# Gathering new and old cache rows in the other order, with filler rows in place of skipped ones

## The reference, cut to what matters

```
k = rope(rms(x @ Wk)), v = x @ Wv                     # 64 new rows for each sequence
k_blocks[block_of(pos), :, pos % 16] = k              # written into the paged cache
v_blocks[block_of(pos), :, pos % 16] = v
k_all, v_all = k_blocks[block_tables], v_blocks[block_tables]
scores = q . k_all / 16, allowed where pos - 256 < kpos <= pos
x = x + softmax(scores) @ v_all @ Wo
```

## Time and profile before

| | us |
|---|---|
| median of 3 runs | 442.44 |
| lowest and highest run | 441.16, 442.81 |
| span of the profiled execution | 494.4 |
| PE busy in it | 444.6 (90%) |
| DVE, POOL, ACT busy in it | 311.1, 268.9, 230.2 |
| DMA rate, mean over the span | 140 GB/s |
| q0, the queue of POOL's gathers | 22.08 MB, 16.5% of 16 engines |

### The profile page before, as it was taken

One profiled execution on the slowest core, in us unless ns is written; L12 is line 12 of the kernel. 1 busy time (PEld: TensorE's weight loads), 2 busy tenths in 40 slices (PEclk: granted clock), 3 DMA queues, 4 the chain that ended last, 5 costly groups with the idle time before them and its releaser, 6 DMA issues.

```text
span 494.4 us, 9866 instructions
## 1 busy us (share of the span) xinstructions
PE 444.6 (90%) x2890; PEld 320.9 (65%) x2890; DVE 311.1 (63%) x901; ACT 230.2 (47%) x590; POOL 268.9 (54%) x241
## 2 busy tenths in 40 slices
PE   5999999996898999989799989897979898989997
PEld 2434468453666777767577767685858675767776
DVE  4988885682646666747465757565647565666543
ACT  1322113653445555646355646554445554555541
POOL 2598157487364756555546556556555556554000
PEclk9999999999799999999989999999999999999999
DMA  6396859755346544453434445353534453434111
GB/s 199 109 302 197 296 170 288 271 144 167 85 110 179 141 115 143 115 147 99 136 100 142 113 143 129 111 147 106 149 88 122 123 141 82 123 104 109 47 54 44
DMA packets 76266, 69.08 MB, mean 140 GB/s; under 512 B 50516, under 2 KB 52692, under 8 KB 76214
## 3 DMA queue, kind: packets, MB, share of 16 engines
q1 hardware_dynamic: 57248, 42.03, 28.7%
q0 software_dynamic: 15456, 22.08, 16.5%
q10 hardware_dynamic: 3510, 4.35, 2.4%
HBM read 78.39 MB, written 11.93 MB: 183 GB/s over the span
## 4 chain that ended last, share of the span: by engine, by line
PE 71%; DVE 11%; issue 9%; ACT 4%; another core or an unknown queue 3%; DMA 2%; ACTq 0%; DVEq 0%; SPq 0%
PE banks L1112 27%; PE banks L1244 8%; PE banks L1125 7%; PE banks L1279 7%; PE banks L1252 5%; PE banks L1106 5%; PE banks L1264 5%; DVE prob L974 3%; DVE x L887 2%; PE banks L1226 2%; ACT x L662 2%; PE banks L1292 2%; DMA kvb<-kvl_dram 1%; PE banks L1378 1%
## 5 line engine op out<-in xcount | busy, mean ns | idle before, releaser
L514 POOL DMA_INDIRECT windows<-kvrows_dram,idx_all x78 | 82.6, 1059 | 63.7 <-PE banks L1264 29.0
L634 ACT ACTIVATE pt_s<-banks 112x384 f32<-112x384 f32 x128 | 57.7, 498 | 96.5 <-PE banks L1252 70.9
L514 POOL DMA_INDIRECT windows<-newkv,idx_all x78 | 79.4, 1019 | 27.6 <-issue 22.4
L974 DVE CUSTOM_DVE_ANT_0 prob<-banks,mask 128x336 f32<-128x336 f32 x128 | 58.5, 505 | 52.1 <-issue 22.4
L628 ACT ACTIVATE prob<-prob,negmax 128x336 f32<-128x336 f32 x128 | 72.4, 567 | 32.3 <-DVE negmax L974 18.3
L484 POOL TENSOR_TENSOR rstd<-ms,half 128x8 f32<-128x8 f32 x24 | 45.9, 1913 | 66.4 <-DVE ms L907 46.2
L1125 PE MATMUL banks<-wkv_s,xt_s 128*128 128x512 f32 x128 | 58.7, 616 | 5.6 <-DMA xt_s<-xt_dram 5.6
L1252 PE MATMUL banks<-cst,prob 128*112 128x128 f32 x384 | 52.7, 273 | 0.2
L1264 PE MATMUL banks<-pt_s,windows 112*64 112x128 f32 x624 | 41.8, 281 | 10.6 <-ACT pt_s L634 8.7
L1112 PE MATMUL banks<-wf_hi,x 128*128 128x512 f32 x120 | 41.7, 408 | 10.5 <-DVE x L887 10.5
L1244 PE MATMUL banks<-kt_s,qt_s 64*128 64x336 f32 x256 | 47.5, 471 | 2.8 <-issue 2.8
(11 more groups left out here) (212 smaller groups left out, 825.0 us busy)
## 6 DMA issues: line engine op xcount, KB each, us to landing
usel<-utab SPq DMA_DIRECT2D x64, 128.0 KB
xt_s<-xt_dram SPq DMA_DIRECT2D x31, 256.0 KB
newkv<-kvo SPq DMA_DIRECT2D x16, 256.0 KB
stage<-xtok_dram SPq DMA_DIRECT2D x16, 256.0 KB
tsel<-ttab SPq DMA_DIRECT2D x64, 64.0 KB
out_dram<-xo ACTq DMA_DIRECT2D x15, 256.0 KB
windows<-kvrows_dram,idx_all POOLq DMA_INDIRECT x78
windows<-newkv,idx_all POOLq DMA_INDIRECT x78
```

What stands on the lines that cost most here:

```text
L514: P.indirect_dma_start(kv_s[i][:, c, :], None, newkv if new else kvrows, bass.IndirectOffsetOnAxis(ap=idx_all[:, new * CH + c, b:b + 1], a ...
L634: A.activation(pt_s[g][:], tb[g % 2][0:KP, 0:CH * 128].rearrange("p (c q) -> p c q", c=CH), ACT.Copy).then_inc(S["pt_ev"], 1)
L974: V.tensor_tensor_reduce(out=prob[b % 3][:, g, :], in0=sbk[g][:, 0:WK], in1=mask[b % 2][:], scale=-1.0 / 16, scalar=3.0e38, op0=ALU.add, o ...
```

## The change

`index_rows` gives every old window row of the sequences 2 to 31 a filler index into `newkv` (a row number spread over that table by the block number) in place of an index out of bounds. For the sequences 0 and 1 (`EARLY`) the skipped rows stay. The old indices are as before, so the old gathers still skip the rows that are new. Since a filler row must be overwritten by the old one, the new half is issued first and the old half after it has landed, except for sequences 0 and 1. In iteration k POOL now waits for `pv_mm` to reach k, then waits until the new half of k + 3 has landed, and then issues the old half of k + 3 and the new half of k + 4 by turns; `root_query` follows in even iterations.

```
-                for i in range(2):
-                    h = slice(HR * i, HR * i + HR)
-                    w = bank[6 + i][0:BLOCK, 0:HR]
-                    has = (qrot, qt_s[0])[i][0:BLOCK, 0:HR]
-                    V.tensor_scalar(none[:, h], w, 0.0, float(NONE), ALU.is_equal, ALU.mult)
-                    link(V.tensor_scalar(has, w, 0.0, float(NONE), ALU.is_gt, ALU.mult))
-                    V.tensor_tensor(rows[:, 1, h], w, none[:, h], ALU.add)
-                    link(V.scalar_tensor_tensor(has, blkrow[0:BLOCK, h], float(BLOCK), has, ALU.mult, ALU.add))
+                parts = [(slice(HR * i, HR * i + HR), bank[6 + i][0:BLOCK, 0:HR], (qrot, qt_s[0])[i][0:BLOCK, 0:HR]) for i in range(2)]
+                for h, w, has in parts:
+                    V.tensor_scalar(has, w, 0.0, float(NONE), ALU.is_gt, ALU.mult)
+                    last = V.tensor_scalar(other[:, h], blkrow[0:BLOCK, h], SPREAD, con("off1", BLOCK), ALU.mult, ALU.add)
+                link(last)
+                first = other.rearrange("p (s b) -> p s b", b=NB)[:, :, 0:EARLY]
+                link(V.tensor_scalar(first, first, float(NONE), None, ALU.add))
+                for h, w, has in parts:
+                    V.scalar_tensor_tensor(other[:, h], w, 0.0, other[:, h], ALU.is_equal, ALU.mult)
+                    last = V.scalar_tensor_tensor(has, blkrow[0:BLOCK, h], float(BLOCK), has, ALU.mult, ALU.add)
+                link(last)
+                for h, w, has in parts:
+                    V.tensor_tensor(rows[:, 1, h], w, other[:, h], ALU.add)
                     last = V.tensor_scalar(rows[:, 0, h], has, con("off", BLOCK), None, ALU.add)
...
+            def half_landed(b):
+
+                pool.wait_ge(kv_in[b % WINDOWS], 96 * (b // WINDOWS) + 48)
...
-            gather(0, 1)
-            gather(1, 1)
-            gather(2, 0)
-            gather(2, 1)
-            gather(3, 0)
+            for b in range(EARLY):
+                half_landed(b)
+                for c in range(CH):
+                    gather(b, 1, c)
+            for b in range(EARLY, 4):
+                for c in range(CH):
+                    gather(b, 1, c)
+            half_landed(2)
+            for c in range(CH):
+                gather(2, 0, c)
...
-                    gather(4, 0)
-                    continue
-                if k + 2 < NB:
-                    gather(k + 2, 1)
-                if k + 4 < NB:
+                if k and k + 4 < NB:
                     pool.wait_ge(S["pv_mm"], k)
-                    gather(k + 4, 0)
-                if k % 2 == 0 and k // 2 + 1 < TILES:
+                if k + 3 < NB:
+                    half_landed(k + 3)
+                    for c in range(CH):
+                        gather(k + 3, 0, c)
+                        if k + 4 < NB:
+                            gather(k + 4, 1, c)
+                if k and k % 2 == 0 and k // 2 + 1 < TILES:
                     root_query(k // 2 + 1)
```

More of the change, by code:

```diff
@@ L26 @@
 SHIFT = 271
+EARLY = 2
+SPREAD = (NB * NT - BLOCK - 1) / (NPOOL - 1)
 WIN_COLS = 32 * WS
@@ L31 @@
 _WIDTHS = [[("ident", 128), ("same_batch", 128), ("of3", NE3)],
-           [("order", NW * NW * NB), ("off", 1), ("toff", NW * BLOCK), ("code", 1), ("ones", NB)],
+           [("order", NW * NW * NB), ("off", 1), ("off1", 1), ("toff", NW * BLOCK), ("code", 1), ("ones", NB)],
            [("inv", 32), ("tpos", 1), ("win", 1)]]
@@ L60, in constants @@
     put("off", np.arange(BLOCK)[:, None])
+    put("off1", np.arange(1, BLOCK + 1)[:, None])
     put("win", (NSLOT * b)[:, None])
@@ L129, in build @@
         later = part(NB, NW * NW * NB // 2, f16).rearrange("p (j n) -> p j n", j=NW)
-        none = blkd[0:BLOCK, 0:WIN_COLS]
+        other = blkd[0:BLOCK, 0:WIN_COLS]
         assert at[0] <= 4 * CH * 512
@@ L507, in _, with gather @@
             root("k", 6, 0)
-            def gather(b, new):
+            def gather(b, new, c):
                 i = b % WINDOWS
[L511 to L518, removed]
+                P.indirect_dma_start(
+                    kv_s[i][:, c, :], None, newkv if new else kvrows,
+                    bass.IndirectOffsetOnAxis(ap=idx_all[:, new * CH + c, b:b + 1], axis=0),
+                    bounds_check=NB * NT if new else NPOOL * BLOCK - 1, oob_is_err=False,
+                ).then_inc(kv_in[i], 16)
+            def half_landed(b):
+                pool.wait_ge(kv_in[b % WINDOWS], 96 * (b // WINDOWS) + 48)
             root("k", 7, 0)
@@ L522, in _ @@
             root("q", 1, 1)
-            gather(0, 0)
+            for c in range(CH):
+                gather(0, 0, c)
             root("k", 8, 0)
-            gather(1, 0)
+            for c in range(CH):
+                gather(1, 0, c)
             pool.wait_ge(S["row0_stored"], 16)
@@ L541, in _ @@
                     pool.wait_ge(S["comb_ev"], NE3 // 2)
-                    gather(4, 0)
-                    continue
-                if k + 2 < NB:
-                    gather(k + 2, 1)
-                if k + 4 < NB:
-                    pool.wait_ge(S["pv_mm"], k)
-                    gather(k + 4, 0)
-                if k % 2 == 0 and k // 2 + 1 < TILES:
+                if k and k + 4 < NB:
+                    pool.wait_ge(S["pv_mm"], k)
+                if k + 3 < NB:
+                    half_landed(k + 3)
+                    for c in range(CH):
+                        gather(k + 3, 0, c)
+                        if k + 4 < NB:
+                            gather(k + 4, 1, c)
+                if k and k % 2 == 0 and k // 2 + 1 < TILES:
                     root_query(k // 2 + 1)
```

## The result

The changed kernel takes 514.16 us (median of 4 runs, 513.13 to 515.38) against 442.26 (4 runs, 441.16 to 442.81). The ratio is 1.1615, 95% interval 1.1574 to 1.1656: 72 us slower. The forecast was 460 (432 to 484). The sign was right; the loss was predicted four times too small.

What follows compares the result with a forecast made beforehand. PE was taken to bound the kernel, gathers hidden; POOL would become the slower loop through landing waits, +17 us, plus indices +0.7: +18 on 442.4 gives 460 us, range 432 to 484 (the forecast's own 450 to 478).

Steps and rivals of the forecast that it cites:

- PE needs 21.5 us a pair: PE's loop: one even and one odd iteration estimated at 10.8 + 10.7 us from the last two iterations.
- late wake-ups: ACT and POOL resume late after PE during gathers with many skipped rows: 2.7 us a pair, little or nothing unprofiled.
- I take 2.75 + 1.1 = 3.85: POOL's wait per iteration: landing plus signalling and start, bounds 3.1 to 5.2 us; POOL pair 22.7, +17 us in all.
- The root fits beside the landing: POOL's loop: the root operation's 2.25 us would fit within the 3.85 us from last gather to next.
- Directly, it costs nothing; it makes each landing later: Filler rows on q0: 16.7 MB more, about 50 GB/s on top of about 120, with room on average.
- Startup order: 0, bounds -0.5 and +1.: Gathers before the loop: about 3.9 of a 5.24 us wait filled, but what follows is gated elsewhere, so 0.
- Indices, +0.7.: `index_rows` on DVE: 13 instructions in place of 10, paid in full through PE, +0.7 us, bounds 0 and +1.3.
- Rival 1: Late resumption after PE's signals also occurs unprofiled, so removing skipped rows gains, down to 427 us; chance 0.22.
- Rival 2: Landings of 2.0 us keep POOL's pair at 21.2, below PE's; only index work remains, 443 us; chance 0.15.
- Rival 3: Bandwidth: six full gathers in a row lengthen landings to 4.1 us and beyond, pair 25.5, 498 us; chance 0.13.
- Rival 4: Filler indices are out of bounds and rows still skipped, leaving the landing wait alone, about 455 us; chance 0.02.
- signs that the prediction named: New trace: POOL landing waits of 1 to 3 us, late `rstd`, pair 22 to 23, no "remote" waits, L1226 never waiting.

Runs made afterwards that it cites:

- second trace of before: Kernel before, unchanged, profiled a second time: span 440.8 us at a time of 442.89 us.
- experiment 1: Changed kernel with all overwritten old rows skipped again in the new halves, order and waits as changed: 496.29 us, ratio 1.1205 to the kernel before.
- experiment 3: Changed kernel with each `usel` load, a broadcast of outermost size 2, cut into two loads of 16 rows: 487.77 us, ratio 1.0992 to the kernel before.
- experiment 11: Changed kernel with most of SP's `xt` left out from tile 4, of `xtok` and `usel` from tile 2; gathers as changed: 474.35 us.
- experiment 10: Changed kernel with overwritten rows skipped and `usel` loads of 16 rows, gather order as changed: 470.69 us, ratio 1.065 to the kernel before.
- experiment 4: Changed kernel with `root_query` after the fourth gather of an even iteration in place of after the sixth: 541.3 us, ratio 1.2238 to the kernel before.
- Experiment 6: Changed kernel with the new half of k + 4 issued before the wait and old half of k + 3, and `usel` loads of 16 rows: 442.58 us.
- experiment 13: Kernel before, unchanged, profiled again: 442.89 us (one run), span 440.8, 20.6 us a pair of iterations, no "remote" wait.
- experiment 2: Changed kernel with the new half of k + 4 issued first, then the landing wait and old half of k + 3: 457.44 us, ratio 1.0336.

## Why the prediction was wrong

*Its start, "PE needs 21.5 us a pair".* Measured 20.6 in the second trace of before. The prediction argued rightly that the late wake-ups are not in the runs. But it tied them to gathers with skipped rows, and experiment 1 and the second trace of before have such gathers and no late wake-up. And it put the pair together from pieces of the last two iterations, and came out 0.9 too long. This alone makes its own sum too small: (22.7 - 20.6) x 14 = 29 in place of 17, so 472, inside its range and still 42 short.

*The term that failed, "I take 2.75 + 1.1 = 3.85" for the gap between the last gather and the next.* The mechanism (POOL waits for what it issued last, and becomes the slower loop) was right; the size was wrong. Behind odd iterations the gap is 3.5 in the mean, mostly 3.2: there the estimate was even high. Behind even ones it is 5.6 to 8.6. The pair has about 10.4 us of gaps where the forecast had 7.7, and takes 25.7 in place of 22.7. So the loss of 5.1 us a pair is the forecast's 1.2, 2.7 of longer gaps, 0.9 of PE's shorter pair, and 0.3 of gathers (15.3 in place of 15.0). The bound of 5.2 for one gap was exceeded behind every even iteration from 2 on. The prediction took landings from two old halves and asked only about the mean DMA share. It did not ask what SP issues at that moment: `usel` on two engines, then `xt` and tokens. Experiments 3 and 11 take these away one after the other (10 takes away `usel` and the filler rows); with small loads the gaps are 3.2 and 3.5, and the pair of 21.9 is even a little under the forecast's 22.7.

*"The root fits beside the landing."* Right: experiment 4, which takes it from there, costs 27.

*"Directly, it costs nothing; it makes each landing later"* (bytes). Right in both halves. q0 moved 15.0 MB more (37.10 against 22.08; 16.7 were forecast). Experiment 6 carries them for nothing, experiment 1 against the changed kernel shows 18 us where landings are waited for.

*"Startup order: 0, bounds -0.5 and +1."* Wrong: iterations 0 to 4 take 23.1 us more than before, where the forecast's 1.2 us a pair gives 2.4. The replaced wait did shrink, to 1.45 us at 99.41, and the root of iteration 0 comes 5.0 us sooner. But then the new wait already acts, at a time when SP stores tables and loads tiles. POOL, DVE and PE in the changed kernel, iterations 1 and 2:

```profile
117.50 0.98 POOL L514 DMA_INDIRECT wpt_late<-kvrows_dram,idx_all  x1 [4.15 <-DMA wpt_late<-newkv,idx_all]
...
131.79 0.99 POOL L514 DMA_INDIRECT windows<-kvrows_dram,idx_all  x1 [6.84 <-PE banks L1281]
...
139.27 1.67 POOL L487 TENSOR_TENSOR rstd<-ms,half 128x8 f32<-128x8 f32 x1
141.03 0.69 DVE L932 TENSOR_TENSOR qrot<-t,rstd 128x512 f32<-128x512 f32 x1 [9.52 <-issue]
141.78 1.12 PE L1155 MATMUL banks<-cst,qrot 128*128 128x128 f32 x4 [9.08 <-DVE qrot L932]
```

The 6.84 is put down to PE, but the second values product, for which this wait stands, ended at 120.3; the last new gather was issued until 124.95, so it is the landing. Experiment 3 shows this: there the same wait is 3.52, put down to the landing, and over at 129.52, before PE's third values product ends (130.60 + 1.53). So `usel` on two engines is part of the early loss too: the root of iteration 4 begins at 160.6 in experiment 3 and at 166.9 in the changed kernel. Then six gathers go ahead of the root, and PE stands 9.08 us. In the second trace of before the same root begins at 130.1.

*Indices, +0.7.* Right: +0.6 in the trace, +1.2 (0.3 to 2.0) in the runs.

*The rivals.* Rival 1 (late wake-ups are real) is refuted by experiment 13. Rival 2 (the wait fits) fails, since even with landings near their shortest experiment 10 is 29 us slower than before. Rival 3 had the right mechanism, landings of 4 us and more beside other traffic, and its 498 was the nearest number; but the cause is less the gathers' own bandwidth than SP's loads, since the odd landings are short with the same gathers, and in experiment 11 the even ones too. Rival 4 fails by q0's bytes. Of the signs that the prediction named, the waits of POOL for landings and the idle DVE before `qrot` came (the waits longer than forecast, the pair 25.7 and not 22 to 23), and PE still waits for no window; that the "remote" waits are gone says nothing, since the second trace of before has none either. By the rule of the Trainium skill that the prediction weighed ("DMA: Bandwidth & Descriptors", "Anatomy of one DMA — SWDGE (gpsimd) path"), nothing would have been lost beyond the indices; the trace disagrees, with about 3.0 us (experiment 10) to 3.2 (changed kernel, experiment 11) from the last gather's end to the next gather's start at the best, where an estimate from that rule and the 1.1 of signalling made 2.6.

## What to carry to other kernels

A wait for a transfer that was issued last on the same engine puts the landing into that engine's loop; issuing the next batch ahead of the wait took 57 of 72 us away with the same bytes. Before costing a landing, list what the other queues issue in the same microseconds and over how many engines each spreads: a DMA share of 0.13, while someone waits, can be two engines that hold everyone up. And profile a kernel a second time when its span and its runs disagree.

## What the hardware showed

- The same program had profiled spans of 494.4 and 440.8 us; its runs were all between 440.8 and 445.7. The "remote" waits of the earlier trace rows came with the first alone.
- A gather of 112 rows takes POOL 0.99 us and 0.30 to the next, with rows skipped or not (experiments 1 and 2).
- PE's granted clock fell in PE's wait (0.75 in the mean from 132.70 to 141.78) and came back late. Windows of the changed kernel around its wait of 9.08 us (the columns as in the fence of windows in experiment 3; the third number from the end is the granted clock):

```profile
128.00:132.00 4.00, 4.00 (x43) 3.01 (x42) 2.49 (x9) 2.60 (x9) 0.21 (x1) 1.00 0.24 65
...
141.78:144.00 2.22, 2.22 (x11) 2.22 (x12) 2.10 (x7) 1.01 (x2) 0.00 (x0) 0.50 0.30 79
144.00:147.00 3.00, 3.00 (x12) 2.61 (x11) 0.62 (x1) 1.95 (x4) 1.06 (x1) 0.50 0.36 93
147.00:150.00 3.00, 3.00 (x23) 2.54 (x21) 0.78 (x4) 0.03 (x1) 2.16 (x3) 0.93 0.86 261
```

  For 5 us behind the wait it is 0.50, the level of 1.2 GHz, while PE is busy all the time. The mean over the span is 0.947, against 0.999 in the second trace of before. Since POOL's sum for a pair above has no wait for PE or DVE in it, I take this as a consequence and not as the cause; no run separates it.
